# Attention with heads of 16: the last 26 keys of four groups as sixteen 32x32 products in one step

## The reference, cut to what matters

```python
q = (x @ Wq).reshape(B, N, 16, 16).transpose(0, 2, 1, 3)          # B = 2, N = 1024
k = (context @ Wk).reshape(B, M, 16, 16).transpose(0, 2, 1, 3)    # M = 154
v = (context @ Wv).reshape(B, M, 16, 16).transpose(0, 2, 1, 3)
attn = softmax(einsum('bhid,bhjd->bhij', q, k) * 16 ** -0.5)
out = einsum('bhij,bhjd->bhid', attn, v)
```

## Time and profile before

| what | us |
|---|---|
| median of 3 runs | 1545.22 |
| lowest, highest | 1532.24, 1550.62 |
| the profiled execution | 1543.91 |
| its span in the profile | 1542.1 |
| mean granted clock of TensorE | 0.904 of full speed |
| attention of layer 0 (chunks) | about 69 to 205 |
| attention of layer 2 (chunks) | about 699 to 862 |
| attention of layer 3 (chunks) | about 1104 to 1240 |

### The profile page before, as it was taken

How to read it: one execution, slowest core, us unless ns; L and a number is a source line. 1 busy time by engine, 2 the same in 40 slices (tenths; PEclk the granted TensorE clock), 3 DMA queues, 4 the chain that set the end, 5 groups by cost and what they waited for, 6 DMA issues and landing times.

```text
span 1542.1 us, 18540 instructions
## 1 busy us (share of the span) xinstructions
PE 1314.2 (85%) x6487; PEld 812.8 (53%) x6513; DVE 711.5 (46%) x2010; ACT 474.8 (31%) x890; POOL 301.6 (20%) x373
## 2 busy tenths in 40 slices
PE   5999979959999856499989869994789877999997
PEld 2645444334565542354544559994544444666664
DVE  5755353386323458876563532223436464122214
ACT  1144434411222216304434113331364321222220
POOL 5200010023000010424022322222242215122220
PEclk9699989969999887769999669997799779999999
DMA  9990010010000010010000456665000022344425
GB/s 263 285 279 1 1 52 0 0 59 0 1 0 1 0 32 0 1 19 1 1 29 28 148 167 211 214 208 184 2 1 22 21 71 95 121 160 151 136 82 172
DMA packets 106201, 124.12 MB, mean 80 GB/s; under 512 B 15138, under 2 KB 90654, under 8 KB 106110
## 3 DMA queue, kind: packets, MB, share of 16 engines
q1 hardware_dynamic: 99118, 104.05, 22.9%
q0 software_dynamic: 6992, 18.88, 3.3%
HBM read 74.05 MB, written 48.86 MB: 80 GB/s over the span
## 4 chain that ended last, share of the span: by engine, by line
PE 74%; DVE 12%; issue 5%; POOL 4%; ACT 3%; DMA 1%; SPq 1%; DVEq 0%; POOLq 0%; ACTq 0%
PE bank L1133 9%; PE bank L726 5%; PE bank L1167 5%; PE bank L1209 4%; PE bank L1176 4%; PE bank L800 4%; PE bank L709 4%; PE bank L820 4%; PE bank L991 3%; PE bank L838 3%; PE bank L849 3%; PE bank L852 2%; PE bank L667 2%; PE bank L901 2%; POOL x_slots L1626 2%
## 5 line engine op out<-in xcount | busy, mean ns | idle before, releaser
L1280 ACT ACTIVATE scratch<-bank 128x512 f32<-128x512 f32 x240 | 126.4, 603 | 96.1 <-PE bank L827 44.2
L1133 PE MATMUL bank<-scratch 128*128 128x320 f32 (+3 forms) x480 | 154.0, 478 | 0.6 <-issue 0.6
L1599 POOL TENSOR_SCALAR rstd<-mv 128x4 f32<-128x4 f32 x36 | 10.2, 284 | 669.0 <-DVE mv L1716 644.4
L1936 DVE TENSOR_REDUCE scratch<-bank 128x2 f32<-128x308 f32 x256 | 105.7, 472 | 72.0 <-PE bank L800 69.7
L1133 PEld LDWEIGHTS bank<-scratch 128*128 128x128 f32 (+1 forms) x480 | 87.1, 185 | 61.3 <-issue 30.2
L2437 DVE TENSOR_TENSOR scratch<-scratch,bank 128x320 f32<-128x320 f32 (+3 forms) x60 | 31.4, 526 | 177.9 <-PE bank L1133 174.6
L1249 ACT ACTIVATE scratch<-bank 128x512 f32<-128x512 f32 x56 | 32.0, 599 | 222.4 <-PE bank L667 222.2
L1626 POOL DMA_INDIRECT x_slots<-scratch x64 | 66.7, 1042 | 106.3 <-DVEq L2294 88.5
L667 PE MATMUL bank<-ident,scratch 128*128 128x128 f32 x224 | 41.9, 349 | 52.9 <-DVE scratch L1722 34.5
L726 PE MATMUL bank<-weights,scratch 128*128 128x256 f32 x320 | 79.9, 409 | 6.2 <-ACT scratch L1344 2.7
L820 PE MATMUL bank<-scratch 32*128 32x512 f32 x384 | 82.2, 649 | 2.3 <-ACT scratch L1325 1.8
(11 more groups left out here) (372 smaller groups left out, 2300.1 us busy)
## 6 DMA issues: line engine op xcount, KB each, us to landing
scratch<-in_L_ffn_W SPq DMA_DIRECT2D x47, 512.0 KB
x_slots<-zeros SPq DMA_DIRECT2D x1, 17680.0 KB, 72.1
scratch<-y_back SPq DMA_DIRECT2D x16, 512.0 KB, 8.0
scratch<-in_L_ffn_w_gate SPq DMA_DIRECT2D x16, 352.0 KB
scratch<-in_L_ffn_w_up SPq DMA_DIRECT2D x16, 352.0 KB
x_slots<-zeros SPq DMA_DIRECT2D x1, 5200.0 KB, 89.0
scratch<-x_slots SPq DMA_DIRECT2D x39, 130.0 KB, 3.1
y_back<-zeros SPq DMA_DIRECT2D x1, 4352.0 KB, 38.7
```

The lines of the kernel that those rows point to most:

```text
L1133: last = pe.matmul(bk[0:fn, 0:n], w[s][:, k, m * P:m * P + fn], moving(k), start=k == 0, stop=k == DK - 1)
L1280: act.activation(v["PT"][:, n % 2, j, :], bk[:], ACT.Exp, scale=float(v["hd"]) ** -0.5).then_inc(RP.read, 1)
L1936: dve.tensor_reduce(v["mx"][:, TPC * c + t, r, 2 * m:2 * m + 2], bk[:, 0:2 * M].rearrange("p (e k) -> p e k", k=M), AX.X, ALU.max)\
```

## The change

The last keys of the four groups of a chunk are one step. It stands once per chunk, in group 0, behind the values product of the group before. `Kr` holds each head's 26 keys once, in 32 columns, in that head's row band. Head j of group g is a 32x32 product from rows 32j to 32j+31 into column band j XOR g of bank g: sixteen products, each on a piece of the array of its own, and in layers 0 and 2 sixteen more with `selxr`. The exponentials go to a new tile `PR`, four banks in a row. `Vr` is laid out to match (band q of group g holds head q XOR g), so that VectorE writes six pieces per batch item and not four. GpSimd's four masked products in a layer become one copy. Tiles in the scratch move, as do `ye` and `yk` of layer 3's experts.

```diff
@@ steps16
-                    o.append(("rem", c, g))
                     o += top[1:2]
                     if g == 3 and has_max and c + 1 < NC:
                         o.append(("negm", c + 1))
                     if n:
                         o.append(("av", *divmod(n - 1, 4)))
+                    if g == 0:
+                        o.append(("rem", c))
                     if g == 0 and ahead:
                         o.append(("yT", c + 2))
@@ TensorE
                     elif what == "rem":
-                        g = i[0]
-                        m, e = divmod(g, 2)
-                        if g == 0 and c == 0:
+                        if c == 0:
                             pe.wait_ge(kr16_made, LA[L] + 1)
-                        bk = RP.take(pe, p, "s", c, g, 4)
-                        if has_max:
-                            pe.matmul(bk[:], selxr[:, g, :, :].rearrange("p j k -> p (j k)"), v["negm"][:, c, :],
-                                      start=True, stop=False)
-                        pe.matmul(bk[:], v["Kr"][:, m, b, e, :, :].rearrange("p j k -> p (j k)"), v["QT"][:, c, m, :],
-                                  start=not has_max, stop=True).then_inc(RP.filled, 1)
+                        bks = []
+                        for g in range(G):
+                            m, e = divmod(g, 2)
+                            bks.append(RP.take(pe, p, "r", c, g))
+                            for j in range(4):
+                                rows, to = slice(32 * j, 32 * (j + 1)), slice(32 * (j ^ g), 32 * (j ^ g) + 32)
+                                last = pe.matmul(bks[g][to, :], v["Kr"][rows, m, b, e, :], v["QT"][rows, c, m, :],
+                                                 start=True, stop=not has_max)
+                            if not has_max:
+                                last.then_inc(RP.filled, 1)
+                        for g in range(G if has_max else 0):
+                            for j in range(4):
+                                rows, to = slice(32 * j, 32 * (j + 1)), slice(32 * (j ^ g), 32 * (j ^ g) + 32)
+                                last = pe.matmul(bks[g][to, :], selxr[rows, g, j, :], v["negm"][rows, c, :],
+                                                 start=False, stop=True)
+                            last.then_inc(RP.filled, 1)
                     elif what == "av":
...
-                        pe.wait_ge(RP.read, RP.n(p, "s", c, g, 4))
+                        pe.wait_ge(RP.read, RP.n(p, "s", c, g, 3) if g else RP.n(p, "r", c, 0))
...
-                            last = pe.matmul(bk[32 * r:32 * (r + 1), :], v["Vr"][:, b, g, r, :],
-                                             v["PT"][:, slot, 4, :], start=False, stop=True)
+                            last = pe.matmul(bk[32 * r:32 * (r + 1), :], v["Vr"][:, b, g, r ^ g, :],
+                                             v["PR"][:, g, :], start=False, stop=True)
@@ ScalarE
+                def last_exponentials(c):
+                    if c:
+                        act.wait_ge(RP.filled, RP.n(p, "av", c - 1, G - 1))
+                    for g in range(G):
+                        bk = RP.get(act, p, "r", c, g)
+                        act.activation(v["PR"][:, g, :], bk[:], ACT.Exp, scale=float(v["hd"]) ** -0.5).then_inc(RP.read, 1)
@@ GpSimd
-                        for m in range(MT):
-                            for b in range(B):
-                                last = pool.tensor_tensor(q["Kr"][:, m, b, :, :, 0:MR],
-                                                          bc(q["Kz"][:, m, b, :, P:M].unsqueeze(2), (P, 2, 4, MR)),
-                                                          bc(quad[:].unsqueeze(1).unsqueeze(3), (P, 2, 4, MR)), ALU.mult)
-                        last.then_inc(kr16_made, 1)
+                        pool.tensor_copy(q["Kr"][:].rearrange("p m b e k -> p (m b e) k")[:, :, 0:MR],
+                                         q["Kz"][:].rearrange("p m b e k -> p (m b e) k")[:, :, P:M]).then_inc(kr16_made, 1)
@@ VectorE, values
+                        for q in range(4):
+                            rows = slice(32 * q, 32 * q + MR)
+                            o = v["Vr"][rows, b, :, q, 0:hd].rearrange("p (m e) d -> p m e d", m=2)
+                            ms = slice(0, 4, 3) if q < 2 else slice(1, 3)
+                            for es, rs in (((slice(0, 2), slice(0, 4, 3)),) if q % 2 == 0 else
+                                           ((slice(0, 1), slice(2, 3)), (slice(1, 2), slice(1, 2)))):
+                                if L >= 2:
+                                    ins = dve.tensor_tensor(o[:, :, es], a[:, ms, rs], bv[:, ms, rs], ALU.add)
+                                else:
+                                    ins = dve.tensor_copy(o[:, :, es], a[:, ms, rs])
+                                st.did(ins)
```

More of the change, by code:

```diff
@@ L337, in build @@
                 v["Vr"] = scratch.take((B, G, 4, v["vw"]))
-            v["PT"] = scratch.take((2, 5, CH))
+            if hd == 16:
+                v["PT"], v["PR"] = scratch.take((2, 4, CH)), scratch.take((G, CH))
+            else:
+                v["PT"] = scratch.take((2, 5, CH))
             if hd == 64:
@@ L352, in build @@
                     v["Kz"] = scratch.take((MT, B, 2, M))
-                    v["Kr"] = scratch.take((MT, B, 2, 4, 32))
+                    v["Kr"] = scratch.take((MT, B, 2, 32))
                     v["av"] = scratch.take((2, CH))
@@ L515, in build @@
                 v["dest"] = scratch.take((E3, 3), U32)
+                v["ye"] = scratch.take((3, 3, D))
                 assert scratch.at <= first_slot
                 scratch.at = far
-                v["ye"] = scratch.take((3, 3, D))
                 v["yk"] = scratch.take((NT, D))
@@ L1271, in attention16, with exponentials @@
                     act.wait_ge(w_loaded[p], 16 * len(loads[p]))
-                def exponentials(c, g, js):
+                def exponentials(c, g):
                     n = c * G + g
-                    if n >= 2 and js[0] == 0:
+                    if n >= 2:
                         act.wait_ge(RP.filled, RP.n(p, "av", *divmod(n - 2, G)))
-                    for j in js:
+                    for j in range(4):
                         bk = RP.get(act, p, "s", c, g, j)
                         act.activation(v["PT"][:, n % 2, j, :], bk[:], ACT.Exp, scale=float(v["hd"]) ** -0.5).then_inc(RP.read, 1)
+                def last_exponentials(c):
[4 more added lines that the diff above has]
+                        act.activation(v["PR"][:, g, :], bk[:], ACT.Exp, scale=float(v["hd"]) ** -0.5).then_inc(RP.read, 1)
                 for what, c, *i in steps16(L):
@@ L1315, in attention16 @@
                     if what == "scores":
-                        exponentials(c, i[0], range(4))
+                        exponentials(c, i[0])
                     if what == "rem":
-                        exponentials(c, i[0], [4])
+                        last_exponentials(c)
                     if what == "av":
@@ new lines, in values @@
+                        at = lambda x: x.rearrange("p (m r d) -> p m r d", m=4, r=4, d=hd)
+                        a, bv = at(bk[0:MR, 0:HD]), at(v["bv"][0:MR]) if L >= 2 else None
+                        for q in range(4):
[6 more added lines that the diff above has]
+                                    ins = dve.tensor_tensor(o[:, :, es], a[:, ms, rs], bv[:, ms, rs], ALU.add)
+                                else:
+                                    ins = dve.tensor_copy(o[:, :, es], a[:, ms, rs])
+                                st.did(ins)
+                            if L == 0:
+                                st.did(dve.tensor_copy(v["Vr"][rows, b, :, q, hd:vw],
+                                                       bc(bk[0:MR, HD:HD + 1].unsqueeze(2), (MR, v["G"], vw - hd))))
+                    else:
+                        a = bk[0:MR, 0:HD].rearrange("p (g j d) -> p g j d", j=4, d=hd)
+                        for j in range(4):
+                            st.did(dve.tensor_copy(v["Vr"][32 * j:32 * j + MR, b, :, j, 0:hd], a[:, :, j]))
```

18 lines of the change are left out of this document (removed).

## The result

| | kernel before | changed kernel |
|---|---|---|
| median of 12 runs each (us) | 1541.09 | 1555.05 |
| lowest, highest | 1532.24, 1550.62 | 1552.42, 1559.29 |
| ratio | | 1.0087, interval 1.0064 to 1.0110 |
| the profiled execution, its span | 1543.91, 1542.1 | 1557.56, 1555.8 |
| its granted clock | 0.904 | 0.898 |

The change costs 0.9%. The forecast was "no difference", -0.6 us on the profiled run. (In the means further down, executions that the record classes as slow are left out: four of the kernel before, with spans of 1555 to 1557.)

The account below looks back on a forecast made before the run. TensorE looked full, but turns with maxima were taken to end with VectorE's chain alongside. Layer 0 +3.2, layer 2 +4.0 and layer 3 -7.8 gave -0.6 us: forecast 1545, no difference, range 1528 to 1562.

Parts of the forecast that it names:

- The step's cost: Layers 0 and 2: the next scores' fourth head waits behind four banks and exponentials, 3.3 us per chunk, 13.4 per layer.
- the first chunk: Layers 0 and 2: no values product ahead, but last keys must wait for all four exponentials, costing 3.5 us.
- The step's cost in layer 3: Layer 3, without selxr: fourth bank read late, 2.4 us in chunk 1, 1.8 in chunk 0, 4.2 in all.
- the "nothing" for chunks 2 and 3: Layer 3: the step's cost there falls into TensorE's idle time behind VectorE and GpSimd work, so nothing.
- Worth 0.1 (four turns) ... 1.0, 0.4 and 0.3: Layer 0's nine turns with maxima: gain from removing last keys, including 0.3 to 0.4 in two turns, sum 2.9 us.
- The shadow: Profiled turn (2,0), layer 0: VectorE's maxima and normalisation run beside TensorE's last keys, both ending at 139.63.
- group 3 turns: Layer 0, chunks 0 to 2: output product and no maxima, so removal gains 1.07 us three times, 3.2.
- last chunk: Layers 0 and 2: last keys and some waiting go, 1.1 us in each of 4 turns, 4.5 per layer.
- rival 3: TensorE's pause at each step takes the clock: 1.7 us in each of ten steps, 17 us, 1562; chance 0.08.
- Rival 1: TensorE is the bound everywhere, so its 34 us come off: 1511, or 1528 for half; chance 0.18 of over 1%.
- rivals 2 and 4: Bands of one bank take turns, 1581, chance 0.06; or groups run one after the other, 1555 to 1560, chance 0.08.
- rival 4: In the step, tile order forces one group after another, 2 to 3 us more each: 1555 to 1560, chance 0.08.

Follow-up runs that it names:

- e7: The changed kernel with the last 26 keys' scores and exponentials left out, the values product adding zeros for them: 1519.89 us, ratio 0.9842 to the kernel before.
- e2: The changed kernel with the sixteen-product step ahead of the values product and five slots for the last exponentials: 1541.66 us, ratio 0.9982 to the kernel before.
- e3: The changed kernel with the four last-keys exponentials covering only 64 of 512 queries: 1539.76 us, ratio 0.9975 to the kernel before.
- e4: The changed kernel with products of which nothing is read added behind the step's sixteen: 1555.53 us, ratio 1.0057 to the kernel before.
- e12: The changed kernel with unread products ahead of the values product in turn 0, chunks 0 to 2, layers 0 and 2: 1549.68 us, ratio 1.0059.
- e6: The changed kernel with the step in two halves, in turns 0 and 2 of each chunk, ahead of the values product: 1537.65 us, ratio 0.9955.
- e10: e7 with unread products added in turns 0 to 2 of chunks 0 to 2, layers 0 and 2: 1525.23 us, ratio 0.9902 to the kernel before.
- e1: The changed kernel with one group's four small products in each turn, in the old place: 1550.64 us, ratio 1.0021 to the kernel before.
- e9: The changed kernel with e6's halves in layers 0 and 2 and e2's whole step in layer 3: 1533.39 us, ratio 0.9951 to the kernel before.

## Why the prediction was wrong, by its steps

**The step's cost: right in layers 0 and 2, a little high.** 13.4 per layer was forecast. Against e7, which has everything but the step, layer 0 of the change costs 123.0 - 110.3 = 12.7, layer 2 146.6 - 134.4 = 12.2. The difference is the first chunk: 3.5 forecast, 2.77 measured (8.42 for 5.65). The turn (2,0) came out at +3.34 for the 3.3 worked out; e2 moved it by 2.5, e3 by 1.49.

**The step's cost in layer 3: too low, by how much is uncertain.** 4.2 forecast; 122.6 - 116.8 = 5.8 as measured, 110.7 - 103.2 = 7.5 with the clock taken out, which holds to some 2 us. In chunks 0 and 1 the sum was right: turns (0,0) and (1,0), at the upper level in both kernels, cost 2.40 (5.30 for 2.90) and 1.90 (7.22 for 5.32), against 1.8 and 2.4. The miss is the "nothing" for chunks 2 and 3: there the step does not fall wholly into the idle time, turn (3,0) is 17.76 in the change and 16.69 in e7.

**"Worth 0.1 (four turns) ... 1.0, 0.4 and 0.3": the step of the order of work that failed.** The turns with maxima were to give 2.9 in layer 0; e7, with no last keys at all, gives 0.6 (0.18, 0.22 and 0.22, six turns nothing). The shadow I had seen in rows 3 is all but complete, in chunk 0 too. The other terms held: group 3 turns 2.9 for 3.2, last chunk 1.1 per turn for 1.1. From the first to the sixteenth turn's exponentials the last keys' removal gives 8.1 in layer 2 (forecast 10.1, or 9.0 without the last turn) and in layer 3 13.2 with the clock taken out, for 13.

**The clock: put at nothing in the sum, and the largest miss.** I had left it to rival 3 because "the wait is shorter, and the products behind it are dense". What the runs show is 14 us more at the lower level, some 7 of the 11 us in the means and 10 of 13.7 in the profiled pair. It is less than half of rival 3's 17, and not where rival 3 put it: in turn (1,0) the fall comes ahead of the step, and filling the pause behind the step (e4) leaves it there. Part of it is settled: turn (1,0) loses 1.6 us in five of six cases, and in e12 a filler ahead of the values product goes with no such loss in both layers and 9 us less at the lower level. The thinned turn is thus part of the cause, but e3's turns (1,0), as thin, keep the upper level, so it is not the whole. Where the remaining difference comes from is open: e2, e6 and e7 (0.8998, 0.8996, 0.8975) have the lower clock too, and in e10 fillers did not bring it back.

**Sum.** Clock taken out, the profiled pair shows layer 0 +6.0 (forecast +3.2), layer 2 +4.1 (+4.0), layer 3 -5.7 (-7.8), with the stretches between them +3.7 (3.8 in the means) against -0.6; the clock adds 10 in this pair, 7 in the means. That layer 2 came out right is in part luck: a gain of 8.1 for 9.0 and a cost of 12.2 for 13.4 cancel. Rival 1 falls (turns with maxima do not shrink even in e7), rivals 2 and 4 too: the 28 passes of L844 run in 1.48 us. That rival 4 had named 1555 to 1560 is a coincidence of size.

**The rule weighed.** The Trainium skill, TensorEngine Tiling (Array Packing), section Gotcha 1: PSUM Pressure, says that row tiles cannot use one bank at the same time. The runs disagree where the row tiles write to different column bands: e1's four row bands into one bank take 1.06 us for eight passes, where one after the other they would take 8 x 0.43 = 3.4.

## What to carry to other kernels

Count a packed step by when its banks come free, not by its products: four banks and four ScalarE reads in a row cost 3.3 us in a middle chunk behind the values product and 0.8 ahead of it, and half a step at a time costs least (over e7 in layer 0, clock taken out: the change 12.7, four in each turn 8.5, the step ahead of the values 6.8, halves 4.5). Before pricing a saving, take the work out altogether (e7): in the turns that VectorE's maxima end, it was worth next to nothing. With scatter of 20 us that is nearly all clock, compare spans less half the time at the lower level too; that splits a 0.9% loss into two parts that the medians mix. It says how large the clock's part is, not what causes it.

## What was not expected of the hardware

- Four 32x32 products side by side take as long as one 128x128 (1.06 and 1.02 us for two passes of 512 columns), eight 1.09.
- Useless products sped the kernel up: e12 has 9 us less at the lower level and is 3 to 4 us faster in mean span.
- The clock's fall came at turn (1,0) in five of six cases with the change's order, in neither of e3's two, and in e6 and e9 at turn (2,1) of layer 0 in both profiles (8.80 and 8.83 us for 7.14), so it seems to follow the kernel's order of work, not chance alone.
